# Second layer's mixer matrix spread over the convolution, message columns paired, transposed copies on ScalarE

## The chip, the cores and the metric

The kernel runs as one program on 1 core of one Trainium2 chip. The metric is the device time of one execution in microseconds, the median of three runs. Of the kernel before these gave 3021.57, 3025.67 and 3026.47 us, median 3025.67 us.

## The reference, cut to what matters

A two-layer graph network on 3125 nodes of 256 features and 53125 edges. The change is in the second layer and in two places that only move a copy. The second layer computes, on normed rows `xn`:

```python
# _L1_gnn_ref: messages of every edge, summed by destination
s0 = src[:, :64]; s1 = src[:, 64:].reshape(-1, 64, 3)
out0 = alpha * (einsum('ei,io->eo', s0 * a0, w_00_0) + inv_sqrt3 * einsum('eim,em,io->eo', s1, a1, w_11_0))
out1 = alpha * (einsum('ei,io,em->eom', s0, w_01_1, a1) + einsum('eim,io->eom', s1 * a0, w_10_1))
messages = concatenate([out0, out1.reshape(-1, 192)]) * msg_rad
agg = segment_sum(messages, edge_dst) / 4
# _L1_mix_ref: linear attention, no softmax
p_attn = einsum('bhnd,bhne->bhde', k, v) / seq_len
out = einsum('bhnd,bhde->bhne', q, p_attn) ... @ Wfc.T + bfc
# x = x + gnn(xn) + mix(xn), then a gated mixture of 4 experts whose gates come from x_norm @ W_gat and a graph attention
```

The mixer is linear in its rows, so it is one 256 x 256 matrix G and one bias row for all nodes; both follow from the Gram matrix of `xn`.

## The kernel before, in words

Nodes lie in NB = 25 blocks of 128 rows (`k.X`, 128 x 25 x 256, stays in SBUF). Each stage is an `nc.Block`: five engines with their own instruction lists, joined by semaphores inside and by a barrier at the end. All products are f32; one f32 product shows as two MATMUL records. The stages that matter here, in order of time:

- `combine0` (L1263), 1003 to 1062 us: per block ScalarE norms the rows (L595), TensorE turns them (L1297), VectorE copies the turned rows out of PSUM (`keep`, L1329), TensorE multiplies by `Ws` (L1307), VectorE scales, adds twice and takes statistics (L1339 to L1343, L475), GpSimd adds the bias (L1289).
- `experts0` (L1380), 1278 to 1524 us: eight experts in turn on TensorE. GpSimd meanwhile sends columns of the sorted pairs for the later gate graph to HBM by indirect DMAs (`Scatter`, L1995, one column each, L2009), paced by expert (`pace`). 281 columns are spread over the stages by `SORT_SCATTER = 6`, `RETURN_SCATTER = 28`, `GRAM_SCATTER = 30`, `MIX_SCATTER = 34` and the end, 36, in units of eight columns: 176 in `experts0`, 16 in `return0`, 32 in `gram1`, 9 in `mixer_matrix1`.
- `gram1` (L2132), 1602 to 1650 us: norms, the table `x_tab` of gather rows, the Gram matrix in `sums`, edge factors; GpSimd issues 4 gathers and 32 scatters. VectorE also clears the accumulator of the next stage (L2229, 128 x 12800).
- `mixer_matrix1` (L2241), 1651 to 1675 us: G and its bias row, five dependent steps of TensorE products and VectorE copies; GpSimd issues the last 9 scatters.
- `convolve` (L2318), 1675 to 2251 us: 55 turns of U = 8 steps of 128 edges. GpSimd gathers 128 source rows per step into a ring of RT = 4 turns (L2345). ScalarE makes `msg` (L2369, L2371), VectorE the one-hot matrix (`mark`, L2383), the products with the three angular factors (`weigh`, L2393), their sum (`join`, L2401, L2403) and the adds of two halves of each step's result into `acc` (`add`, L2413). TensorE does one 128 x 512 product per step (L2358) over R = 4 banks. GpSimd may run up to four turns ahead of the others.
- `combine1` (L2431), 2251 to 2368 us: per block ScalarE copies the sums and norms the rows (L2464, L595); TensorE turns both (L2483 two, L2485 four), multiplies by G (L2496) and by a 512 x 256 matrix `c_w` laid out from the four 64 x 64 weights with zeros between (L2498); VectorE copies both turned tiles (L2537, L2538), adds (L2548), takes statistics. The bias is added by GpSimd (L2473), one block behind each norm, and after block 9 its queue holds the nine gathers of `Steps.gather` (L239). `Steps` prepares the gate graph: `count`, `widen`, `cuts` after block 9, `gather`, `mark` after block 19, `flip`, `settle`.
- `gate_rows` (L2570), 2371 to 2418 us: per block a norm, two transposes (L2611), two copies of the same turned rows (L2639, L2640), a product of 16 columns (L2621), and five small VectorE instructions for the gate scores (L2651 to L2656). SP stores rows and loads expert weights.

The order inside a block that matters most, `combine1` on TensorE:

```python
turned_block(b + 1, (j + 1) % B5)      # waits normed b+1, kept
pe.wait_ge(kept, b + 3)
for c in range(KC): matmul(ps_o[j % 2][:, 0:D], xT[:, j, c, :], G[:, c, :], ...)
for c in range(4):  matmul(ps_o[j % 2][:, 0:D], aT[:, j, c, :], w[:, c, :], ...)
```

## Time and profile before

| | us |
|---|---|
| median of three runs | 3025.67 |
| the profiled execution's own time | 3023.47 |
| its span | 3021.7 |
| PE / DVE / ACT / POOL busy | 2281.1 / 2035.0 / 1375.9 / 1641.5 |
| `combine0` | 58.5 |
| `experts0` | 246 |
| `gram1` + `mixer_matrix1` | 73.8 |
| `convolve` | 575.7 |
| `combine1` | 117.1 |
| `gate_rows` | 46.5 |

Times are microseconds unless marked ns. PE is TensorE's products, PEld its weight loads, DVE VectorE, ACT ScalarE, POOL GpSimd, SP SyncE; "POOLq" and "SPq" are queues. L12 is a line of the kernel before. Stages are separated by barriers, so a microsecond saved on whatever ends a stage moves all that follows.

### The profile page before, as it was taken

The numbers are of one execution on the slowest core, as the hardware profiler recorded it, in microseconds if no ns is written. First come the engines' busy times: TensorE is split into PE (matmuls) and PEld (weight loads), VectorE is DVE, ScalarE is ACT, GpSimd is POOL, SyncE is SP. The second block draws the span as 40 slices with busy tenths as digits, with TensorE's granted clock in tenths as the row PEclk, the third lists the DMA queues.
The fourth block names the chain that finished last, engine by engine and source line by source line (L and its number), as shares of the span: only waits on it lengthen the run. The fifth ranks groups of instructions, "written<-read, shape, count | busy, mean of one in ns | idle before, by whom it ended". The sixth has DMA issues, their size and how long they took to land. (4 is left out here: it accounts for less than half of the span.)

```text
span 3021.7 us, 41600 instructions
## 1 busy us (share of the span) xinstructions
PE 2281.1 (75%) x11076; PEld 1512.9 (50%) x11076; DVE 2035.0 (67%) x4208; ACT 1375.9 (46%) x4369; POOL 1641.5 (54%) x1754
## 2 busy tenths in 40 slices
PE   3997777777777656699965578777778788888785
PEld 2554455555555455556623223222337677777664
DVE  4564899999999888701075699999984722222586
ACT  0221566666666244321242588888972122222232
POOL 1544766666664204567776677777752077777200
PEclk8998788888888855599976799999989689989898
DMA  3212766666664022233232233333321211111004
GB/s 105 54 41 80 217 192 197 195 193 193 195 193 140 1 58 73 58 88 94 87 85 62 82 105 105 103 104 105 105 63 16 61 37 36 32 37 37 17 1 182
DMA packets 165629, 289.12 MB, mean 96 GB/s; under 512 B 55933, under 2 KB 99970, under 8 KB 165407
## 3 DMA queue, kind: packets, MB, share of 16 engines
q0 software_dynamic: 79344, 187.14, 22.8%
q1 hardware_dynamic: 73906, 80.60, 8.6%
q10 hardware_dynamic: 12156, 18.72, 1.7%
q8 instruction: 102, 1.67, 0.2%
q14 instruction: 121, 0.98, 0.1%
HBM read 250.08 MB, written 36.25 MB: 95 GB/s over the span
## 5 line engine op out<-in xcount | busy, mean ns | idle before, releaser
L949 POOL DMA_INDIRECT at_kv<-kv_tab,e_src x440 | 431.9, 981 | 265.5 <-PE at_a L1066 152.4
L2358 PE MATMUL cv_ps<-cv_msg,cv_hot 128*128 128x512 f32 x880 | 431.1, 632 | 145.3 <-DVE acc L2413 126.5
L2345 POOL DMA_INDIRECT cv_x<-x_tab,e_src x440 | 423.7, 963 | 147.7 <-issue 98.8
L2794 POOL DMA_INDIRECT gs_h<-h_tab,fc_q x312 | 295.1, 946 | 184.9 <-issue 93.6
L2358 PEld LDWEIGHTS cv_ps<-cv_msg,cv_hot 128*128 128x128 f32 x880 | 162.0, 198 | 414.1 <-ACT cv_msg L2371 252.6
L2009 POOL DMA_INDIRECT pairs<-gating_pair,gating_place x281 | 275.9, 982 | 149.0 <-issue 66.5
L2371 ACT ACTIVATE cv_msg<-cv_x,factors 128x64 f32<-128x64 f32 x1320 | 356.5, 333 | 0.0
L2413 DVE TENSOR_TENSOR acc<-acc,cv_ps 128x256 f32 x880 | 306.9, 412 | 6.5 <-PE cv_ps L2358 3.8
L2369 ACT ACTIVATE cv_msg<-cv_x,factors 128x256 f32<-128x256 f32 x440 | 217.8, 495 | 122.6 <-DMA cv_x<-x_tab,e_src 122.6
L1066 PE MATMUL at_a<-at_kv,at_hot_e 128*128 128x264 f32 x880 | 252.9, 416 | 13.9 <-ACT at_hot_e L993 9.9
L1041 PE MATMUL at_q<-q_parts,at_hot_n 128*128 x1320 | 228.2, 329 | 42.5 <-DVE at_hot_n L1128 21.1
L2751 ACT ACTIVATE gs_x_hid<-gs_x_h,x_b 128x128 f32<-128x128 f32 x320 | 91.5, 369 | 303.9 <-PE gs_x_h L2718 303.9
L2728 PE MATMUL gs_x_y<-x_w,gs_x_hid 128*128 128x256 f32 x640 | 171.6, 419 | 51.6 <-DVE gs_y L2758 51.5
L1041 PEld LDWEIGHTS at_q<-q_parts,at_hot_n 128*128 128x128 bf16 x1320 | 147.3, 113 | 112.7 <-issue 61.2
L1066 PEld LDWEIGHTS at_a<-at_kv,at_hot_e 128*128 128x128 f32 x880 | 163.7, 207 | 47.3 <-ACT at_hot_e L993 19.0
L1003 ACT ACTIVATE at_kv<-at_kv 128x32 f32<-128x32 f32 x864 | 185.6, 306 | 0.0
L1167 DVE TENSOR_TENSOR acc<-acc,at_a 128x528 f32 x220 | 154.0, 700 | 39.5 <-PE at_a L1066 31.9
L2871 DVE TENSOR_REDUCE gs_as_dst<-gs_d 128x32 f32<-128x96 f32 x39 | 10.1, 258 | 250.7 <-DMA gs_h<-h_tab,fc_q 250.7
L2728 PEld LDWEIGHTS gs_x_y<-x_w,gs_x_hid 128*128 128x128 f32 x640 | 128.7, 210 | 73.7 <-issue 46.9
L2718 PE MATMUL gs_x_h<-xnT,x_w 128*128 128x128 f32 x1280 | 161.0, 283 | 0.0
L2718 PEld LDWEIGHTS gs_x_h<-xnT,x_w 128*128 128x128 f32 x1280 | 157.9, 199 | 2.7
L1138 DVE TENSOR_TENSOR at_kv<-at_kv,at_q 128x512 f32<-128x512 f32 x220 | 147.2, 680 | 15.9 <-DVE at_ends L1240 6.1
(546 smaller groups left out, 4437.9 us busy)
## 6 DMA issues: line engine op xcount, KB each, us to landing
x_space<-in_L_ffn_w SPq DMA_DIRECT2D x16, 1024.0 KB, 7.0
at_rel_row<-e_rel_rows SPq DMA_DIRECT2D x55, 256.0 KB, 4.5
experts_out<-gs_y ACTq DMA_DIRECT2D x20, 512.0 KB, 2.7
x_y<-experts_out SPq DMA_DIRECT2D x20, 512.0 KB, 6.9
at_kv<-kv_tab,e_src POOLq DMA_INDIRECT x440, 3.7
cv_x<-x_tab,e_src POOLq DMA_INDIRECT x440, 2.8
kv_tab<-p_qkv SPq DMA_DIRECT2D x25, 256.0 KB, 2.0
gs_h<-h_tab,fc_q POOLq DMA_INDIRECT x312, 2.4
```

The source lines that it names most:

```text
L949: nc.gpsimd.indirect_dma_start(out=kv[:, t % (RING * Q4), 0:2 * D], out_offset=None, in_=kv_tab, in_offset=bass.IndirectOffsetOnAxis(ap=e. ...
L1041: ins = nc.tensor.matmul(ps_q[dd % 3][:, u, :], hot_n[:, t // Q4 % NHOT, t % Q4 * P:(t % Q4 + 1) * P], q_parts[:, ds(b, 1), n, :].rearrang ...
L1066: nc.tensor.matmul(to, hot_e[:, t // Q4 % NEDGE, t % Q4, :], kv[:, t % (RING * Q4), D:2 * D + H1], start=(u == 0), stop=(u == 1), skip_gro ...
L2009: nc.gpsimd.indirect_dma_start(out=pairs, out_offset=bass.IndirectOffsetOnAxis(ap=place_i[:, c:c + 1], axis=0), in_=pair[:, c, :], in_offs ...
L2345: nc.gpsimd.indirect_dma_start(out=xg[:, i % RT, u, :], out_offset=None, in_=x_tab, in_offset=bass.IndirectOffsetOnAxis(ap=e.src[:, t:t + ...
L2358: nc.tensor.matmul(ps[u % R][:, :], hot[:, i % 2, u, :], msg[:, i % 2, u, :], start=True, stop=True).then_inc(summed, 1)
L2369: nc.scalar.activation(msg[:, h, u, 0:D], xg[:, i % RT, u, :], ACT.Copy, scale=factor[:, t:t + 1, 0])
L2371: ins = nc.scalar.activation(msg[:, h, u, D + m * M:D + (m + 1) * M], xg[:, i % RT, u, 0:M], ACT.Copy, scale=factor[:, t:t + 1, 1 + m])
L2413: v.tensor_tensor(row, row, ps[u % R][:, n * D:(n + 1) * D], ALU.add).then_inc(added, 1)
L2718: ins = self.nc.tensor.matmul(self.ps_h[e % 2][:, f * P:(f + 1) * P], self.x1.w1[:, e, c, f * P:(f + 1) * P], self.xnT[:, c, b * P:(b + 1) ...
L2728: ins = self.nc.tensor.matmul(self.ps_y[e % 2][:, 0:D], self.hid[:, e % 2, f, :], self.x1.w2[:, e, f, :], start=(f == 0), stop=(f == FX // ...
L2794: nc.gpsimd.indirect_dma_start(out=hg[:, i % RT, u, :], out_offset=None, in_=h_tab, in_offset=bass.IndirectOffsetOnAxis(ap=e.src[:, i * U ...
```

## The change

Seven parts, all in one diff:

1. `combine0`: the copy of the turned rows moves from VectorE to ScalarE, which norms block b + 1 before it copies block b.
2. Scatters: `RETURN_SCATTER` 28 to 30, so `experts0` issues 192 (16 more); `return0` 16 as before; `gram1` the last 25 (7 fewer); `MIX_SCATTER` is gone.
3. `gram1` no longer clears `acc`; `convolve` does, before its first `mark`.
4. `mixer_matrix1` is gone. A class `NodePart` cuts its work and the product of every block with G into 57 phases (7 for the matrix and the bias, 2 for each block), laid over slots 1 to 105 of 110, two slots a turn. TensorE's part stands after step 3 or 7 of a turn, ScalarE's copy one half turn later, VectorE's add to `k.X` after `add` of step 2 or 5. One PSUM bank serves all.
5. `msg` is laid out in pairs of 64 columns, so each of the four turned tiles of `acc` meets one of two 128 x 64 weights.
6. `combine1`: no norm, no rows turned, no product with G, no copy of `acc` (TensorE turns `acc` directly); four products of 64 columns a block; ScalarE makes the one copy left; four weight loads of DMA instead of eight; GpSimd adds all 25 bias rows first, then gathers; buffers three deep.
7. `gate_rows`: the score weights are multiplied into the 24-column weight once; per block ScalarE makes one copy, VectorE two small ones.

```diff
         def _(act):
-                for i in range(0, NB // B5):
-                    for j in range(B5):
-                        act.wait_ge(turned, i * B5 + j + 1)
-                        normed_block(nc, k, act, i * B5 + j, xn[:, j, :], normed)
...
+                norm(0)
+                for b in range(NB):
+                    norm(b + 1)
+                    act.wait_ge(turned, b + B5 + 1)
+                    if b >= B5:
+                        act.wait_ge(done, b - B5 + 1)
+                    nc.scalar.activation(xT[:, b % B5], ps_t[b % B5 % 2][:, 0:D].rearrange("p (c t) -> p c t", t=P), ACT.Copy).then_inc(kept, 1)
```

```diff
 # scatters, and the head of gram1's and convolve's changes
-RETURN_SCATTER = C2 // U - 8
+RETURN_SCATTER = C2 // U - 6
 GRAM_SCATTER = RETURN_SCATTER + 2
-MIX_SCATTER = GRAM_SCATTER + 4
...
-        scatter = Scatter(s, "g1_sc_", GRAM_SCATTER, MIX_SCATTER)
+        scatter = Scatter(s, "g1_sc_", GRAM_SCATTER, C2 // U)
...
-                v.memset(acc[:, :, :], 0.0).then_inc(emptied, 1)
```

```diff
+class NodePart:
+    MIX = 7
...
+        phases = self.MIX + 2 * NB
+        self.phase_at = {1 + p * (slots - 4) // phases: p for p in range(phases)}
...
+    def multiply(self, pe, slot):
+        p = self.phase_at.get(slot)
+        if p is None:
+            return
...
+        if 0 < p <= self.MIX:
+            pe.wait_ge(self.kept, p)
...
+        elif (p - self.MIX) % 2 == 0:
+            b = (p - self.MIX) // 2
+            pe.wait_ge(self.normed, b + 1)
+            if b:
+                pe.wait_ge(self.added, b)
+            for c in range(KC):
+                ins = nc.tensor.transpose(bank[:, c * P:(c + 1) * P], self.xn[:, b % 2, c * P:(c + 1) * P], k.ident[:, :])
+        else:
+            b = (p - self.MIX) // 2
+            pe.wait_ge(self.kept, self.MIX + b + 1)
+            for c in range(KC):
+                ins = nc.tensor.matmul(bank[:, D:2 * D], self.xT[:, b % 2, c, :], self.G[:, c, :], start=(c == 0), stop=(c == KC - 1))
+        ins.then_inc(self.made, 1)
+    def keep(self, act, slot):
...
+        if p < self.MIX or (p - self.MIX) % 2 == 0:
+            act.wait_ge(self.made, p + 1)
...
+    def add(self, dve, slot):
...
+        dve.wait_ge(self.made, p + 1)
+        self.nc.vector.tensor_tensor(self.k.X[:, b, :], self.k.X[:, b, :], self.bank[:, D:2 * D], ALU.add).then_inc(self.added, 1)
```

```diff
 # convolve: TensorE, ScalarE, VectorE
                         nc.tensor.matmul(ps[u % R][:, :], hot[:, i % 2, u, :], msg[:, i % 2, u, :], start=True, stop=True).then_inc(summed, 1)
+                        if u == 3:
+                            node.multiply(pe, 2 * i)
+                    node.multiply(pe, 2 * i + 1)
...
+                        parts = msg[:, h, u, :].rearrange("p (r x i) -> p x r i", x=2, i=M)
...
+                        if u == 3:
+                            node.keep(act, 2 * i - 1)
+                    node.keep(act, 2 * i)
...
+                node.clear()
+                v.tensor_copy(angles, factor[:, 0:T1, 1:4]).then_inc(kept, 1)
                 v.tensor_copy(counted, k.count_row[:, 0:P]).then_inc(kept, 1)
-                dve.wait_ge(kept, 2)
+                v.memset(acc[:, :, :], 0.0).then_inc(kept, 1)
+                dve.wait_ge(kept, 3)
...
                     add(i, blocks, 1, 2)
+                    node.add(dve, 2 * i - 1)
                     join(i + 1)
-                    add(i, blocks, 3, 4, 5, 6, 7)
+                    add(i, blocks, 3, 4, 5)
+                    node.add(dve, 2 * i)
+                    add(i, blocks, 6, 7)
```

```diff
 # combine1
+                for b in range(NB):
+                    act.wait_ge(turned, b + 1)
+                    if b >= 3:
+                        act.wait_ge(done, b - 2)
+                    nc.scalar.activation(aT[:, b % 3], ps_a[b % 3][:, :].rearrange("p (c t) -> p c t", t=P), ACT.Copy).then_inc(kept, 1)
...
                 for b in range(NB):
-                    pool.wait_ge(normed, b + 1)
...
+                    nc.gpsimd.tensor_tensor(k.X[:, b, :], k.X[:, b, :], bias, ALU.add).then_inc(biased, 1)
+                st.gather(pool)
...
+                def mix(b):
+                    pe.wait_ge(kept, b + 1)
+                    if b >= 3:
+                        pe.wait_ge(added, 2 * (b - 2))
+                    for c in range(4):
+                        ins = nc.tensor.matmul(ps_o[b % 3][:, c * M:(c + 1) * M], aT[:, b % 3, c, :], w[:, min(c, 1), :], start=True, stop=True,
+                                               skip_group_check=True)
+                    ins.then_inc(done, 1)
...
+                for b in range(NB):
+                    turn(b + 2)
+                    mix(b)
+                    if b == B5 - 1:
+                        st.widen(pe)
+                    if b == 4 * B5 - 1:
+                        st.flip(pe)
...
 # gate_rows
+                for b in range(NB):
+                    turned_block(b + 2)
+                    pe.wait_ge(kept, b + 1)
...
+                    for c in range(KC):
+                        ins = nc.tensor.matmul(ps_h[b % B5][:, 0:GW + H2], xnT[:, c, b * P:(b + 1) * P], w[:, c, :], start=(c == 0),
+                                               stop=(c == KC - 1))
...
+                    dve.wait_ge(done, b + 1)
+                    v.tensor_copy(h[:, j, :], ps_h[j][:, 0:GW]).then_inc(ready, 1)
+                    v.tensor_copy(as_dst[:, b, :], ps_h[j][:, GW:GW + H2]).then_inc(taken, 1)
```

## Rows read from the trace of the kernel before

**Rows 1.** Busy time by stage; columns: stretch, its length, PE, PEld, DVE, ACT, POOL, PEclk, DMA share, GB/s
```profile
1003.00:1061.50 58.50, 39.93 (x152) 28.27 (x151) 54.98 (x127) 14.33 (x25) 18.47 (x25) 0.85 0.00 1
...
1601.70:1650.60 48.90, 29.07 (x124) 22.79 (x124) 31.23 (x64) 14.60 (x25) 35.73 (x36) 0.78 0.25 74
1650.60:1675.50 24.90, 20.42 (x48) 10.65 (x48) 3.89 (x15) 0.00 (x0) 8.65 (x9) 0.56 0.01 1
...
1700.00:2200.00 500.00, 382.70 (x788) 143.59 (x788) 467.41 (x985) 445.42 (x1581) 379.75 (x395) 0.97 0.36 104
...
2251.20:2368.30 117.10, 90.76 (x460) 78.04 (x460) 56.47 (x135) 27.59 (x50) 26.31 (x34) 0.88 0.09 13
...
2371.50:2418.00 46.50, 36.48 (x152) 29.75 (x152) 37.95 (x181) 14.32 (x25) 0.00 (x0) 0.50 0.36 96
```

**Rows 2.** `combine0`, groups: shapes, count | busy, mean ns | idle before, releaser
```profile
L1329 DVE COPY c_xT<-c_t 128x256 f32<-128x256 f32 x25 | 10.1, 408 | 0.0
```

**Rows 3.** `experts0` on POOL, in order of time: start, length, what
```profile
1292.24 0.96 POOL L2009 DMA_INDIRECT pairs<-gating_pair,gating_place  x1 [0.71 <-PE x_h L1448]
...
1519.04 0.96 POOL L2009 DMA_INDIRECT pairs<-gating_pair,gating_place  x1 [0.30 <-issue]
1524.13 0.10 POOL L1544 MEMSET re_top<- 128x1 f32 x1 [4.13 <-POOLq L1400]
```

**Rows 4.** `gram1`, `mixer_matrix1` and the start of `convolve` on POOL
```profile
1638.84 0.96 POOL L2009 DMA_INDIRECT pairs<-gating_pair,gating_place  x1 [0.31 <-issue]
...
1647.69 0.96 POOL L2009 DMA_INDIRECT pairs<-gating_pair,gating_place  x1 [0.31 <-issue]
1651.19 0.96 POOL L2009 DMA_INDIRECT pairs<-gating_pair,gating_place  x1 [2.54 <-SPq L2257]
...
1676.16 0.98 POOL L2345 DMA_INDIRECT cv_x<-x_tab,e_src  x1 [13.88 <-SPq L2336]
```

**Rows 5.** VectorE at the end of `gram1` and the start of `convolve`
```profile
1630.10 10.72 DVE L2229 MEMSET acc<- 128x12800 f32 x1 [2.62 <-issue]
...
1675.54 2.00 DVE L2414 COPY cv_factors<-factors 128x1760 f32<-128x1760 f32 x1 [0.58 <-PEq L2257]
...
1687.78 1.76 DVE L2393 TENSOR_TENSOR cv_s1w<-cv_x,cv_factors 128x1536 f32<-128x1536 f32 x1 [8.79 <-DMA cv_x<-x_tab,e_src]
```

**Rows 6.** `convolve` from 1800 to 2000, groups, columns as in the second group
```profile
L2345 POOL DMA_INDIRECT cv_x<-x_tab,e_src x159 | 153.6, 966 | 48.5 <-issue 35.7 <-ACT cv_msg L2371 12.2 <-DVE cv_s1w L2393 0.6
...
L2393 DVE TENSOR_TENSOR cv_s1w<-cv_x,cv_factors 128x1536 f32<-128x1536 f32 x20 | 35.1, 1754 | 10.7 <-DMA cv_x<-x_tab,e_src 10.6
```

**Rows 7.** `combine1` on PE, in order of time
```profile
2260.77 1.06 PE L2485 MATMUL c_a<-ident,c_ac 128*128 128x128 f32 x4
...
2269.58 0.60 PE L2485 MATMUL c_a<-ident,c_ac 128*128 128x128 f32 x4
2270.01 1.03 PE L2496 MATMUL c_o<-G,c_xT 128*128 128x256 f32 x4
...
2347.11 0.90 PE L231 MATMUL s_turned<-ident,s_scratch 128*128 128x128 f32 x3 [5.79 <-DVEq L305]
```

**Rows 8.** `combine1`, who waited for whom: total, times, longest
```profile
DVE X L2548 <- POOL X L2473: 10.2, 1, 10.2
```

**Rows 9.** Busy time and granted clock, columns as in the first group, of three short stretches
```profile
2261.00:2263.00 2.00, 2.00 (x11) 1.76 (x10) 1.09 (x3) 1.12 (x2) 2.00 (x4) 0.50 0.00 0
2263.00:2265.00 2.00, 2.00 (x10) 1.78 (x10) 1.90 (x4) 1.12 (x2) 2.00 (x4) 1.00 0.00 0
1080.00:1090.00 10.00, 9.48 (x89) 9.19 (x87) 8.62 (x13) 7.57 (x20) 0.00 (x0) 0.50 0.28 62
```

**Rows 10.** `gate_rows` on PE, one block back to back, in order of time
```profile
2380.55 0.87 PE L2621 MATMUL gr_ps_h<-gat_w,gr_xT 128*128 128x16 f32 x4
2381.27 0.67 PE L2611 MATMUL gr_t<-ident,gr_xn 128*128 128x128 f32 x2
```

**Rows 11.** Expert products of the gate stage on PE
```profile
2500.28 1.95 PE L2718 MATMUL gs_x_h<-xnT,x_w 128*128 128x128 f32 x16
```

More of the change, by code:

```diff
@@ L2320, in convolve @@
+def convolve(nc, k, e, x_tab, factor, sums, acc, spaces):
     turns = T1 // U
@@ L2398, in join @@
                         return
[L2399 removed]
+                    last = msg[:, i % 2, :, M:2 * M]
                     dve.wait_ge(freed, i + 1)
```

426 lines of the change are left out of this document (185 added, 241 removed).

## The prediction

> **What bounds the kernel now.** I read the busy time by stage first [rows 1], since a mean over 3021.7 us hides five different limits, then the order of time at each stage's start and end, then who waited for whom. Each touched stage ends on another engine. `combine0` is VectorE's: 54.98 of 58.50 us busy [rows 1]. `experts0` is TensorE's, but GpSimd has little room: its scatters go at 0.96 + 0.30 = 1.26 us each, and the last began 5.1 us before the next stage [rows 3]. `gram1` ends on GpSimd: its last scatter begins at 1647.69, and the next block's first scatter 3.50 us later [rows 4], while VectorE's late work is a memset that ends at 1640.8 [rows 5]. `mixer_matrix1` is a chain of small steps in which TensorE is busy 20.42 of 24.90 us at clock 0.56 [rows 1]. `convolve` is GpSimd's: 159 gathers took 153.6 us of work and 35.7 us of issue, with only 12.8 us of waits for the other engines, (153.6 + 48.5) / 159 = 1.27 us each or 10.17 us a turn; ScalarE and VectorE start turns by waiting for gathered rows (10.6 us of such waits on VectorE in 200 us) [rows 6]. `combine1` is TensorE's once it runs (2.00 of 2.00 us busy at clock 1.00) [rows 9], plus gaps of which the largest single one is 10.2 us in which VectorE waits for bias rows that stand behind nine gathers in GpSimd's queue [rows 8]. `gate_rows` is VectorE's and TensorE's at clock 0.50 [rows 1].
>
> **The change, part by part.** *`combine0`.* VectorE loses 25 copies of 0.408 us [rows 2], 10.2 us of busy time. Pipelined they are worth less, because an instruction's start overlaps the end of the last: I take 0.33 each, 8 us. ScalarE has 14.33 us busy in 58.5 [rows 1] and takes 10 more without becoming the limit. TensorE does 39.93 / 25 = 1.6 us a block at clock 0.85 against the 1.8 that VectorE keeps. Gain 8, between 4 (TensorE at half clock in more blocks) and 10.
>
> *Scatters.* `experts0` gets 16 more. Its fourth scatter begins at 1292.24 [rows 3]; the other 188 at 1.264 each (the seven steps from 1638.84 to 1647.69 in rows 4) put the last at 1529.9 if nothing paces them. The pace doesn't help or hurt: 24 scatters take 30.3 us, an expert takes (1519.04 - 1292.24) / 173 x 22 = 28.8. So GpSimd, hidden until now, ends the stage: 1529.9 + 3.5 [rows 4] = 1533.4 against 1524.13 [rows 3], a loss of 9. Between 0 (if half of them were to find gaps, which no row shows) and 12. `gram1` has seven fewer: its last begins where the 25th does now, 1638.84 instead of 1647.69 [rows 4], a gain of 8.9, provided VectorE doesn't end it; the memset leaves it, so its copies of the sums, now at 1640.7 behind the memset that began at 1630.10 [rows 5], come 10.7 us earlier. The nine of `mixer_matrix1` vanish with it.
>
> *`mixer_matrix1`.* The whole block goes: 24.9 us [rows 1]. What it did is paid for inside `convolve`.
>
> *`convolve`.* The path is GpSimd's 440 gathers, which the change doesn't touch; the others have room, and a ring of four turns decouples them. Load per turn of 10.17 us, old from rows 1 (500 us are 49.2 turns), new by division over 55 turns: VectorE 467.41 / 49.2 = 9.5, plus 25 adds of 0.42 = 0.2, so 9.7. ScalarE 445.42 / 49.2 = 9.05, plus 25 norms of 14.32 / 25 = 0.57 [rows 1] and 25 copies at about 0.41 [rows 2] and the matrix's seven, 0.5, so 9.6. TensorE 382.70 / 49.2 = 7.8, plus the matrix, 20.42 x 0.56 = 11.4 us at full clock [rows 1], and 25 times two transposes (0.22) and four records of 256 columns (1.03) [rows 7], 0.8 in all, so 8.6. All stay under 10.17, the nearest by 0.5. The waits that the phases add: ScalarE waits for TensorE's phase, with `msg` of the next steps behind it, for which TensorE waits; it stands half a turn after the phase and I find it late by up to 2 us, made up in the next turn that has no copy. TensorE's transposes wait for VectorE's add of the block before, with the next products behind them; 48 of the 56 distances between phases are two slots, where the add is long done. The memset of 10.72 us now precedes the first `mark`: VectorE's start at 1675.54 leaves 12.2 us until the first rows are there [rows 5], of which copies and `mark` take 3.5, so it is late by some 2 us, and the first phases by up to 8. Both are lags of the consumers, not of GpSimd, and at 0.5 us a turn they are gone after 20 of 55 turns. I cost the stage at 0. If that cover is gone, every 0.1 us over 10.17 costs 5.5. Bounds -2 (no row gives the gathers less work) to +60.
>
> *`combine1`.* Four DMAs instead of eight let the weights in about 5 us after the stage's start, not 9. A block then is four transposes, 2270.01 - 2269.58 = 0.43 us [rows 7], and eight records of 64 columns. No row has these at full clock: 128 columns take 1.95 / 16 = 0.12 [rows 11], which is the upper bound; at half clock 16 columns take (2381.27 - 2380.55) / 4 = 0.18 [rows 10], which halved is 0.09. I take 0.10, nearer to the wide one, so 1.25 us a block against about 3.25 now. VectorE has two small adds and statistics, about 1.0; ScalarE one copy, 27.59 / 50 = 0.55 [rows 1]. Measured from the stage's start: weights 4.7; three blocks of transposes and one of products at half clock 4.0; 19 blocks at 1.25 and `widen`, 24.5: block 19 is done at 33.2. After block 9, at 21.7, `cuts` takes 2.5; nine gathers at 1.26 and a landing of about 2 us put the windows at 37.5, so now `mark` waits for the gathers, not for the blocks: this is what becomes late next. Bias rows are no longer behind them. `mark` 4.8, `flip` at half clock 1.4, the last five blocks 6.9 (TensorE has stood still and starts slowly, as at 2347.11 [rows 7]), and 2 us of VectorE: 52.5. Gain 117.1 [rows 1] - 52.5 = 64.6.
>
> The LDWEIGHTS section of the Trainium skill's page "TensorE: Matmul & The Clock Gate" puts a weight load at columns / 1.2 ns, 107 ns for 128. By that estimate a block is 1.29 us and the stage 1 us longer; no row here separates the two.
>
> *`gate_rows`.* VectorE falls from seven instructions a block to two of about 0.17; then TensorE's 2 transposes and 4 records at half clock, 0.72 [rows 10] and 0.45, set 1.17 us a block. ScalarE has a norm and a copy, 0.9. With 3 us of start and 2 of end, 34.5 against 46.5 [rows 1]: gain 12, between 8 (a store behind 1 MB of weights) and 16 (if the clock rises).
>
> **Sum.** 8 - 9 + 8.9 + 24.9 - 0 + 64.6 + 12 = 109.4. The profiled execution took 3023.47 us, 2.2 below the median of the runs; 3023.5 - 109.4 = 2914.
>
> **Rivals.** *Half clock in `combine1`.* In a stretch of the router with transposes and products of 8 columns TensorE was busy 9.48 of 10 us and the clock stayed at 0.50 [rows 9]; narrow products may not lift it, and the new stage has 64 columns where it had 256. Then a block is 0.86 (1.06 for four with its tail [rows 7]) + 8 x 0.18 = 2.3 us, block 19 is done at 53, the stage ends at 71: 18.7 later, 2933 us. Against it: the step from 0.50 to 1.00 at 2263.0 came when TensorE had done nothing but transposes since 2260.3 [rows 7, 9], and the new stage begins with twelve of them. The same page's section on the PE-mode transpose says that transposes don't count as activity; by that rule the rival would be likelier than not. The row at 2263.0 speaks against that rule, so I leave it at 0.17.
>
> *`convolve` becomes VectorE's.* Order matters more than load: a phase in which TensorE waits for an add or VectorE for a late product costs VectorE time. It decides from (10.17 - 9.7) x 55 = 26 us in all. With 1 us lost at each of 57 phases the turn is 10.7, the stage 31 longer, 2945. For it: slack of 5%; against: banks are refilled four steps ahead, and VectorE's adds stand after the phase. 0.17.
>
> *Slower than before.* Same place, but each phase empties the pipeline: ScalarE, TensorE and VectorE hand one bank round, and `msg`, the products and `acc`'s adds stand behind every hand-over. At 3 us a phase (a product, a copy, an add and their signals) 171 us go to 55 turns, 3.1 each; 9.7 + 3.1 = 12.8 a turn, 145 us more, 3059. It turns the gain round from 2.4 us a phase. Only 0.03, since two slots, 10 us, lie between a phase and the next.
>
> *More than forecast*: records of 64 columns at 0.06, `gate_rows` at full clock, scatters that find room: 2896. 0.08.
>
> **How the numbers follow.** The forecast has 0.55, its own range 2903 to 2927 from the bounds of `combine0`, scatters and `gate_rows`. The range takes in the half clock whole and the near half of `convolve`'s rival, and at the low end half of the extra gain: 2898 to 2946. About 0.2% (6 us) is what a measurement of this kernel can tell from no change; only the last of the slow cases and small mishaps of unnamed size reach it: faster 0.96, same 0.01, slower 0.03.
>
> **What would show it.** `experts0` with GpSimd's last scatter near 1530 and TensorE idle before the barrier; `gram1` ending some 9 us sooner; the first convolution gather at about 1676 - 8 + 9 - 34 = 1643; 10.1 to 10.2 us between the starts of `weigh` with waits for DMA on VectorE after some 20 turns; in `combine1` a granted clock of 1.00 until `mark` and POOL's gathers as VectorE's releaser; 1.17 us a block in `gate_rows`. Wrong if GpSimd waits for `weigh` or for ScalarE in `convolve` for more than the 12.8 us per 200 of now, or if `combine1`'s clock stays at 0.50.

## The result and the profile after

The changed kernel takes 2924.66 us (median of four runs, 2923.32 to 2928.94) against 3025.35 us: a ratio of 0.9674, 95% interval 0.9659 to 0.9688. The forecast was 2914, the range 2898 to 2946. The gain is 100.7 us, 8.7 less than worked out.

Its profiled execution has a span of 2921.6 us. First the stages: stretch, its length, then busy time of PE, PEld, DVE, ACT and POOL with counts, granted clock, DMA share, GB/s. They stand in the order `combine0`, `experts0`, `gram1`, 500 us of `convolve`, `combine1`, `gate_rows`; most of them answer to [rows 1].

```profile
1002.20:1053.70 51.50, 35.22 (x150) 26.62 (x150) 48.89 (x102) 21.17 (x50) 19.44 (x25) 0.86 0.00 1
1274.00:1524.60 250.60, 229.42 (x832) 150.35 (x832) 23.52 (x48) 42.79 (x64) 181.95 (x190) 0.96 0.29 84
1602.00:1644.00 42.00, 27.73 (x124) 22.09 (x124) 21.09 (x66) 14.48 (x25) 28.88 (x30) 0.83 0.28 86
1700.00:2200.00 500.00, 397.13 (x946) 167.18 (x945) 473.34 (x1005) 462.19 (x1631) 380.56 (x393) 0.99 0.36 104
2221.70:2282.00 60.30, 38.40 (x309) 37.50 (x309) 33.87 (x111) 15.15 (x26) 26.09 (x34) 0.80 0.17 23
2282.00:2318.00 36.00, 30.72 (x152) 29.78 (x152) 8.68 (x62) 22.38 (x51) 0.00 (x0) 0.50 0.51 130
```

The table compares marks that both traces have (first and last starts of named instructions), so that each stretch holds a stage with its barrier.

| stretch | before | after | change | forecast |
|---|---|---|---|---|
| `combine0`, bias copy to last add | 57.9 | 51.1 | -6.7 | -8 |
| `experts0`, first product to next stage | 240.7 | 250.7 | +10.0 | +9 |
| `gram1` and `mixer_matrix1`, to the first convolution gather | 74.4 | 41.8 | -32.6 | -33.8 |
| `convolve`, first gather to last add | 574.6 | 577.3 | +2.7 | 0 |
| `combine1`, to the first product of `gate_rows` | 120.9 | 60.6 | -60.2 | -64.6 |
| `gate_rows` | 48.1 | 36.0 | -12.1 | -12 |
| the rest of the kernel behind it | 601.95 | 603.6 | +1.6 | 0 |

The rows add up to 97.3 of the 100.1 us between the two profiled spans; the other 2.8 lie ahead of `experts0`, outside `combine0`, where nothing was edited. The last row holds no edit either; in the kernels run below, most of which leave it alone too, it was 600.0 to 607.2. What lies ahead of `experts0` varied between 1272.3 and 1279.0 us in kernels that have this part unchanged. So single stages are compared by their own marks; only sums of several microseconds are read from the medians.

`experts0` ends on GpSimd. On POOL (start, length, what, and in brackets the idle time before it and what ended it) three rows, and under them TensorE's last work in the stage and the first behind it:

```profile
1281.01 0.96 POOL L2010 DMA_INDIRECT pairs<-gating_pair,gating_place  x1 [10.24 <-PE x_h L1450]
...
1522.06 0.96 POOL L2010 DMA_INDIRECT pairs<-gating_pair,gating_place  x1 [0.30 <-issue]
1524.62 0.10 POOL L1546 MEMSET re_top<- 128x1 f32 x1 [1.60 <-POOLq L1402]
...
1495.17 14.08 PE L1459 MATMUL x_y<-x_space,x_hid 128*128 128x256 f32 x64 [0.76 <-ACT x_hid L1479]
1524.81 2.09 PE L2099 MATMUL re_ef_h<-ef_emb,ef_w 20*128 20x512 f32 x8 [15.56 <-PEq L1402]
```

TensorE is done at 1509.3 and stands still for 15.6 us while the last scatters go out. Also to be seen: GpSimd waited 10.24 us for TensorE ahead of its third scatter (issued at 1281.01).

`combine1`, rows of TensorE and VectorE:

```profile
2226.55 2.82 PE L2542 MATMUL c_a<-ident,acc 128*128 128x128 f32 x12 [5.71 <-DVE c_w L2568]
2229.16 1.80 PE L2550 MATMUL c_o<-c_w,c_aT 128*128 128x64 f32 x8
2232.08 0.61 PE L2542 MATMUL c_a<-ident,acc 128*128 128x128 f32 x4
2232.53 1.00 PE L2550 MATMUL c_o<-c_w,c_aT 128*128 128x64 f32 x8
2233.37 0.60 PE L2542 MATMUL c_a<-ident,acc 128*128 128x128 f32 x4
...
2262.63 0.36 DVE L285 CAST s_from_node<-s_edges 128x384 f32<-128x384 int32 x1 [3.92 <-DMA s_edges<-pairs,e_chunk]
...
2267.59 0.90 PE L231 MATMUL s_turned<-ident,s_scratch 128*128 128x128 f32 x3 [10.69 <-DVEq L305]
```

A block takes 2233.37 - 2232.08 = 1.29 us, of which the eight records of 64 columns take 2233.37 - 2232.53 = 0.84, 0.105 each. VectorE then waits 3.92 us for the windows, the edge lists that GpSimd's nine gathers bring, and TensorE stands still for 10.69 us in all until the marked windows can be turned.

### The profile page after: what moved, and what is told of

It is laid out like the page before. It is cut to its first block and busy times, and to the rows that moved or that the text cites. A ratio compares the mean times of both kernels' runs of the same rounds, so it can differ in the third digit from the quotient of the medians.

```text
span 2921.6 us, 41520 instructions
## 1 busy us (share of the span) xinstructions
PE 2224.1 (76%) x11075; PEld 1495.1 (51%) x11076; DVE 1978.0 (68%) x4041; ACT 1396.4 (48%) x4454; POOL 1642.7 (56%) x1754
## 5 line engine op out<-in xcount | busy, mean ns | idle before, releaser
L2413 PE MATMUL cv_ps<-cv_msg,cv_hot 128*128 128x512 f32 x880 | 420.6, 613 | 128.3 <-DVE acc L2475 79.9
L1041 PE MATMUL at_q<-q_parts,at_hot_n 128*128 x1320 | 229.6, 330 | 41.8 <-DVE at_hot_n L1128 21.1
```

Source lines behind the costliest of these rows:

```text
L1041: ins = nc.tensor.matmul(ps_q[dd % 3][:, u, :], hot_n[:, t // Q4 % NHOT, t % Q4 * P:(t % Q4 + 1) * P], q_parts[:, ds(b, 1), n, :].rearrang ...
L2413: nc.tensor.matmul(ps[u % R][:, :], hot[:, i % 2, u, :], msg[:, i % 2, u, :], start=True, stop=True).then_inc(summed, 1)
```

## Experiments

Ratios are to the kernel before, measured beside it; a difference to the changed kernel (0.9674) in microseconds is the difference of ratios times 3025. Each ratio is good to about 5 us either way, a difference of two to about 7. The stretches between marks are good to about 1: `convolve` took 577.2 to 578.5 in the seven profiled kernels that leave it alone, its gathers 559.2 to 560.5. Only `combine1` varies more. In the nine kernels that leave it alone it took 60.0 to 60.9 in six and 65.1 to 65.7 in three (experiments 3, 4 with two copies, and 6), and the clock is what differed; see the rivals in the next section.

### 1. The scatters' split put back

```diff
-RETURN_SCATTER = C2 // U - 6
+RETURN_SCATTER = C2 // U - 8
```

> The changed kernel with only the split of the scatters put back: the expert stage has 176 again instead of 192, and the Gram stage 41 instead of 25. Theory (GpSimd ends both stages, every scatter is worth 1.26 us where it is exposed): the expert stage falls from 250.7 to about 240.7 us, since TensorE's own last product then ends it; the Gram stage, from its first instruction to the convolution's first gather, grows from 41.8 by 16 x 1.26 = 20.2 to 62.0; together 10 us slower than the changed kernel, about 2935. Rival (the 10 us that the expert stage lost come from the traffic of the scatters or from the clock, not from their number at the end): the expert stage stays within 2 us of 250, and the whole is 18 to 20 slower, 2944.

Measured: 0.9713 (0.9697 to 0.9730), 11.8 slower than the changed kernel. `experts0` 240.5, from `gram1` to the first gather 62.0, all else unchanged within 1 us. Both numbers of the theory to 0.2 us. In `gram1`, which GpSimd ends, a scatter costs its 1.26 us whole: 16 of them 20.2. Moved into `experts0`, the same 16 cost 10.2: the last scatter came 12.8 us later in the stage, the rest went into gaps of the paced queue.

### 2. Scatters of `experts0` without the pace

```diff
-                scatter.run(nc, k, pool, pairs, pair, place_i, pace=pace)
+                scatter.run(nc, k, pool, pairs, pair, place_i)
```

> The changed kernel, where the scatters of the expert stage no longer wait for TensorE's marks but are issued as fast as GpSimd can. Theory (with 192 scatters the stage is GpSimd's, and its waits for TensorE, 10.2 us before the third scatter and 7.3 in all after it, are paid in full): the second scatter is at 1269.8, 190 more at 1.264 put the last at 1510, just behind TensorE's last product at 1509.3; the stage ends at 1514 instead of 1524.6, 10.5 us faster, 2914. Rival (the pace protects the experts' row and weight loads from the scatters' traffic): TensorE waits for weights, its last product slips by more than 5 us, and the gain is below 5 or turns into a loss.

Measured: 0.9638 (0.9622 to 0.9654), 10.9 faster than the changed kernel, 2914.24 us. `experts0` takes 240.4 us. Its last scatter and the start of the next stage on POOL, and the stage in one row (columns as in the first table of rows):

```profile
1513.18 0.96 POOL L2010 DMA_INDIRECT pairs<-gating_pair,gating_place  x1 [0.30 <-issue]
1516.55 0.10 POOL L1546 MEMSET re_top<- 128x1 f32 x1 [2.40 <-POOLq L1402]
...
1276.10:1516.50 240.40, 229.41 (x832) 150.48 (x832) 23.51 (x48) 42.84 (x64) 179.65 (x188) 0.98 0.30 88
```

The scatters now start in step with the stage, not 10 us into it, and TensorE's busy time is as before, 229.4: the scatters' traffic slowed nothing that shows. With 192 scatters the stage is as long as with 176 and the pace (240.5 in experiment 1), so the loss that the forecast booked for the 16 scatters was the pace's, not theirs.

### 3. The phases left out of the convolution

```diff
         assert len(self.phase_at) == phases
+        self.phase_at = {}
...
-                dve.wait_ge(node.added, NB)
-                dve.wait_ge(node.kept, node.MIX)
```

> The changed kernel with all 57 phases of the node work left out of the convolution: the mixer matrix and its product with the rows are not computed, and X lacks that part. Theory (the stage is GpSimd's, phases lie in the others' slack): the stretch from the convolution's first gather to its last, 559.8 us, shrinks by no more than the 3.3 that it grew, and the whole is 0 to 4 us faster, 2921 to 2925. Rival (convolution is VectorE's with the phases in, order costs more than load): 10 us or more faster, and GpSimd's waits for ScalarE's messages, 15.5 us in 200, fall to under 5.

Measured: 0.9670 (0.9651 to 0.9689), 1.2 faster. From first to last gather 558.1, to the last add 576.3, so 57 phases cost 1.8 and 1.0 us in a stage of 577, little more than the spread of unchanged kernels. Both profiles from 1800 to 2000, with the phases and without them:

```profile
1800.00:2000.00 200.00, 159.05 (x378) 67.79 (x379) 189.92 (x408) 185.54 (x656) 152.19 (x158) 0.98 0.36 104
```

```profile
1800.00:2000.00 200.00, 148.91 (x316) 54.94 (x315) 186.95 (x393) 177.06 (x629) 152.09 (x158) 0.99 0.36 104
```

Without them PE is busy 10.1 us less, ACT 8.5 and DVE 3.0; GpSimd does what it did.

### 4. One and two more VectorE copies a turn

```diff
+        spare = [s.sb(f"cv_spare{q}", [P, D]) for q in range(2)]
...
                     node.add(dve, 2 * i - 1)
+                    for q in range(1):          # the second kernel: range(2)
+                        v.tensor_copy(spare[q][:, :], held[:, 0:D])
                     join(i + 1)
```

> The changed kernel with one more VectorE copy of 128 x 256 from PSUM in each of the 55 turns of the convolution, about 0.41 us; its target is not read. Theory (a turn of VectorE holds 9.66 of 10.17 us): 10.07 still fits under GpSimd's turn, the stage grows by 0 to 5 us. Rival (VectorE is already the one that sets the turn): 55 x 0.41 = 22 us slower, 2947.

> The changed kernel with two more such copies a turn, 0.82 us. Theory: a turn of VectorE is now 9.66 + 0.82 = 10.48, over GpSimd's 10.17 by 0.31, so the stage grows by 0.31 x 55 = 17 us, and GpSimd's idle time moves from issue to waits for VectorE or ScalarE. Rival (VectorE sets the turn already): 45 us slower. A second rival (starts of instructions overlap, so that there is more room than the busy time says): under 8.

Measured: one copy 0.9704 (0.9687 to 0.9721), last add at 582.7, so 5.4 later (9 by the medians); two copies 0.9716 (0.9699 to 0.9732), last add at 586.3, 9.0 later (13 by the medians). Three `weigh` of the second kernel in a row, where no wait for rows is left:

```profile
1989.97 1.75 DVE L2456 TENSOR_TENSOR cv_s1w<-cv_x,cv_factors 128x1536 f32<-128x1536 f32 x1
...
2000.06 1.74 DVE L2456 TENSOR_TENSOR cv_s1w<-cv_x,cv_factors 128x1536 f32<-128x1536 f32 x1
...
2010.47 1.74 DVE L2456 TENSOR_TENSOR cv_s1w<-cv_x,cv_factors 128x1536 f32<-128x1536 f32 x1
```

A turn of VectorE is 10.09 us, and 10.41 with a node add; over the stage that would be 10.24 on average, and a few turns are longer. A copy of 0.41 us costs 0.33 in a row of others, so without the two it is 9.58: the forecast had 9.7. With two copies VectorE ends the stage: 15.9 us to the first `weigh`, 55 turns of 10.24, and a remainder of 7.2 (the longer turns and the last adds, taken from this kernel) make 586.3. Turned round, VectorE ends it from (577.3 - 15.9 - 7.2) / 55 = 10.08 us a turn; the room per turn is 0.50 us (forecast: 0.47). So the theory's mechanism held and its 17 us were too many, by the overlap of starts that the second rival named; that rival's own figure, under 8, was too low. One copy, 9.9 a turn, stays below that point and still cost 5.4 us, just over the theory's 0 to 5. Neither theory has a reason for it; the gathers themselves had grown, to 564.8 from first to last.

### 5. What lengthens the gathers

All 440 gathers in one row each, kernel before, changed kernel, and the one with one copy more (minimum, median, maximum in ns, first and last start):

```profile
L2345 POOL DMA_INDIRECT cv_x<-x_tab,e_src x440: 942/949/1423, 1676.2 to 2232.7; - x147
```

```profile
L2400 POOL DMA_INDIRECT cv_x<-x_tab,e_src x440: 942/946/1459, 1644.0 to 2203.8; - x147
```

```profile
L2401 POOL DMA_INDIRECT cv_x<-x_tab,e_src x440: 942/949/1453, 1648.6 to 2213.4; - x147
```

In none of them is there a gap over 0.35 us between two gathers: GpSimd never waits. What differs are 43 to 53 gathers that take more than 1 us. Their excess over 0.95 sums to 6.4 us before, 10.6 in the changed kernel, 7.6 without phases, 14.7 with one copy more; in seven kernels with this stage unchanged it was 9.9 to 11.3. Of the 5.0 us that one copy added to the gathers' stretch 4.1 are such excess; most of the rest is a median of 0.949 instead of 0.946, whose cause is open. One of them, on POOL, and what VectorE did beside it:

```profile
1853.07 0.95 POOL L2400 DMA_INDIRECT cv_x<-x_tab,e_src  x1 [0.30 <-ACT cv_msg L2431]
1854.32 1.44 POOL L2400 DMA_INDIRECT cv_x<-x_tab,e_src  x1 [0.30 <-issue]
...
1853.54 0.68 DVE L2463 TENSOR_TENSOR cv_msg<-cv_s1w 128x512 f32<-128x512 f32 x1
1854.26 0.69 DVE L2465 TENSOR_TENSOR cv_msg<-cv_msg,cv_s1w 128x512 f32<-128x512 f32 x1
1854.86 1.41 DVE L2475 TENSOR_TENSOR acc<-acc,cv_ps 128x256 f32 x4
```

The gather starts 0.06 us into the second addition of `join` and ends at 1855.76, 0.81 us behind that addition's end at 1854.95. The same holds for all 45 long gathers of the changed kernel: each starts inside one of the two additions of `join`, the only VectorE instructions in the loop with both operands in SBUF (`mark` and `weigh` read one of theirs from PSUM), and ends 0.81 or 0.82 us after that one's end. Fifty-five gathers start inside such an addition. Of the ten that stay at 1 us or under, nine start in its last 0.19 us, where by the same sum little or nothing is left to pay, and one starts together with it. A gather that is under way when an addition begins is not lengthened (42 of them, at most 0.949). Beside `mark`, `weigh`, the adds to `acc` or the clearing of `acc` none is lengthened. So what the stage pays depends on where the joins fall against the gathers, and an edit to VectorE's list can move them. The next kernel tests the link itself.

```diff
-                    v.tensor_tensor(last, s1w[:, :, 0, :], s1w[:, :, 1, :], ALU.add).then_inc(chain, 1)
-                    dve.wait_ge(chain, i + 1)
-                    v.tensor_tensor(last, last, s1w[:, :, 2, :], ALU.add).then_inc(built, 1)
+                    v.tensor_reduce(last, s1w[:, :, :, :].rearrange("p u m i -> p u i m"), AX.X, ALU.add).then_inc(built, 1)
```

> The changed kernel, where VectorE sums the three weighed parts of a message in one reduction over 1536 elements instead of two additions of 512 that each read two operands from SBUF. In every profile so far GpSimd never waits in the convolution; what differs is the time of about 45 gathers that take up to 1.46 instead of 0.95 us, and nearly every one of them overlaps such an addition and ends about 0.1 us behind it (excess of the long gathers: 6.3 us in the kernel before, 10.5 in the changed one, 14.7 with one copy a turn more). Theory (an addition with both operands in SBUF holds GpSimd up, a reduction with one doesn't): the excess goes to under 2 us, the gathers' stretch falls from 559.8 to 551, but VectorE's turn grows by 0.35 to about 10.08, just over GpSimd's 10.02, so that VectorE's last add ends 4 to 7 us earlier, not 9: about 2919. Rival (the reduction holds GpSimd up as well, or the lengthening has to do with VectorE being busy in any way): the excess stays at 8 or more, and the stretch at 558 or longer.

Measured: 0.9660 (0.9642 to 0.9678), 4.2 faster than the changed kernel by the medians, an interval that holds zero. The gathers:

```profile
L2400 POOL DMA_INDIRECT cv_x<-x_tab,e_src x440: 942/946/983, 1646.7 to 2195.6; - x147
```

```profile
1905.58 0.41 DVE L2368 TENSOR_TENSOR X<-X,cv_node 128x256 f32<-128x256 f32 x1
1905.91 1.90 DVE L2463 TENSOR_REDUCE cv_msg<-cv_s1w 128x512 f32<-128x1536 f32 x1
1907.74 3.39 DVE L2473 TENSOR_TENSOR acc<-acc,cv_ps 128x256 f32 x10
...
1800.00:2000.00 200.00, 158.74 (x380) 67.00 (x378) 198.52 (x380) 186.53 (x661) 151.26 (x161) 0.99 0.36 106
```

Not one gather of 440 is longer than 0.983 us, though 74 start inside the reduction alone (at most 0.949), and first to last takes 548.9 instead of 559.8: the cause is shown. Nor is it peculiar to additions. In the first layer's attention, which no run here edits, the changed kernel has 30 gathers (`at_kv`) over 1 us that start inside a multiplication with both operands in SBUF (L1156); they take up to 1.96 us and end 0.81 to 0.82 behind it. In `convolve` the stage gains nothing, since the reduction takes 1.83 in its row where the two additions took 1.33: VectorE, busy 198.52 of 200 us, now ends it at 577.1. Taking 15.9 to the first `weigh` and the remainder of 7.2, its turn is 10.07, as expected. What the expectation (a last add 4 to 7 us earlier) left out was that remainder on top of 55 turns: with it VectorE's own end lies 0.2 us from the end that the long gathers had set.

The Trainium skill's page "SBUF — State Buffer", section "Who interferes with whom", says that a VectorE instruction with two SBUF inputs contends with a GpSimd instruction that reads SBUF, and that a reduction never does; both agree with the 45 gathers and the 0. The same section infers that descriptor generation isn't touched by such an addition; here gathers issued by GpSimd took up to 1.459 instead of 0.946 us, and the measurement decides.

### 6. The clearing of acc back in the Gram stage

```diff
                 v.tensor_copy(sums[0:1, 2, 0:D], ps_row[0:1, 0:D]).then_inc(moved, 1)
+                v.memset(acc[:, :, :], 0.0).then_inc(moved, 1)
                 dve.wait_ge(copied, G1)
-                dve.wait_ge(moved, 1)
+                dve.wait_ge(moved, 2)
...
-                v.memset(acc[:, :, :], 0.0).then_inc(kept, 1)
-                dve.wait_ge(kept, 3)
+                dve.wait_ge(kept, 2)
```

> The changed kernel with the clearing of acc (10.7 us on VectorE) put back into the Gram stage, but behind VectorE's last copies there, at about 1633, where it ends at 1644, beside GpSimd's last scatters. Theory (the cleared accumulator stood ahead of the first weigh, which ran 4 us late, and that lag is what the convolution's last add, 2.7 us later than in the kernel before, shows): the first weigh comes at 11.6 us behind the first gather instead of 15.9, the Gram stage grows by 0 to 2 us, the convolution shrinks by 0 to 3; together between 2 faster and 2 slower. Rival (the lag is caught up at once and the 3.3 us come from the phases): convolution unchanged at 577, and the whole slower by what the Gram stage grows.

Measured: 0.9696 (0.9680 to 0.9712), 6.7 slower. `gram1` grew by 3.8, the first `weigh` came at 11.7, and still the last add came at 581.3, 4.0 later, with 1.4 of it in the gathers. So the late first `weigh` is not why `convolve` grew, and there the rival was right; but it also expected the stage unchanged, which it wasn't. The other 2.6 us fall behind the last gather and weren't settled. `combine1` took 5.0 longer in the profiled execution; its clock rose 12.8 us after the first transpose, where it was 4.3 in the changed kernel.

### 7. Cuts earlier, flip later in combine1

```diff
-                    if b == B5 - 1:
+                    if b == 0:
                         st.widen(pe)
...
                 turn(0)
-                turn(1)
                 st.cuts(dve)
+                turn(1)
                 turn(2)
```

> The changed kernel, where combine1 works out the cuts behind block 4 instead of block 9, and the wide row is spread behind block 0. Nothing is added or removed. Theory (the mark of the windows waits for the gathers, 3.92 us of idle VectorE at 2258.7): GpSimd's nine gathers start when its bias adds end, 2240 instead of 2247, so their windows are there about 2257, and the mark starts right behind block 19: the stage takes 56.8 instead of 60.7, 3.9 faster, 2920.8. Rival (another cost ends the wait, for example the store of the block row on the DMA rings, or GpSimd and VectorE slow each other down when gathers and adds overlap): gain under 1.5.

Measured: 0.9655 (0.9638 to 0.9671), `combine1` 59.4, only 1.3 shorter, though the wait for the windows is gone. The start of `mark` in this kernel, and TensorE from the turn of the windows to its last product, here and in the changed kernel:

```profile
2254.48 0.22 DVE L2575 TENSOR_TENSOR X<-X,c_o 128x64 f32<-128x64 f32 x1 [0.46 <-PE c_o L2550]
2255.22 0.34 DVE L285 CAST s_from_node<-s_edges 128x384 f32<-128x384 int32 x1
...
2260.20:2272.50 12.30, 12.28 (x58) 12.09 (x58) 3.29 (x12) 1.79 (x3) 0.00 (x0) 0.50 0.00 0
```

```profile
2267.60:2276.10 8.50, 8.50 (x58) 8.36 (x58) 3.26 (x12) 1.79 (x3) 0.00 (x0) 0.75 0.00 0
```

The mark starts right behind block 19, 5.1 us earlier in the stage (3.9 expected), but the same 58 records took 12.3 us at a granted clock of 0.50 throughout, where the changed kernel's clock rose on the way and they took 8.5. The clock took back 3.8 of what the wait gave: neither the theory nor its rival had that. That the shorter pause was the reason is not shown. Experiment 3 leaves `combine1` alone, TensorE stood still for 11.6 us ahead of these records, and yet:

```profile
2270.63:2282.96 12.33, 12.32 (x58) 12.13 (x58) 3.29 (x12) 1.79 (x3) 0.00 (x0) 0.50 0.00 1
```

In the other eight kernels with `combine1` unchanged they took 8.0 to 8.9. The next kernel adds the later flip, which leaves TensorE work during the mark:

```diff
-                    if b == 4 * B5 - 1:
+                    if b == 4 * B5 + 2:
                         st.flip(pe)
```

> As the kernel with early cuts, and TensorE turns the marked windows behind block 22 instead of block 19. Theory (TensorE stands still for 10.7 us before the turn although three result banks are free): blocks 20 to 22 are done during the mark, so VectorE adds them as soon as the mark ends, and only 23 and 24 are left: mark from 2258.7 to 2263.5, three blocks of adds at 0.9 each to 2266.2, two more by 2268, the turned windows copied and the last statistics by 2270, against 2278.5: 9 us faster than the changed kernel, 2916. Rival (the last blocks run at half clock whatever the order, because TensorE has stood still before them): 6 us or less.

Measured: 0.9641 (0.9625 to 0.9658), 10.0 faster than the changed kernel; `combine1` 51.8, 8.8 shorter, as the theory had it. With three blocks done before the flip, it doesn't matter that the last two are slow.

```profile
2269.65 0.55 PE L231 MATMUL s_turned<-ident,s_scratch 128*128 128x128 f32 x3 [1.94 <-DVEq L305]
...
2269.76 0.22 DVE L2575 TENSOR_TENSOR X<-X,c_o 128x64 f32<-128x64 f32 x1 [0.21 <-DVE e_src L300]
```

### 8. Products 256 wide in combine1

```diff
-        w = s.sb("c1_w", [P, 2, M])
+        w = s.sb("c1_w", [P, 2, D])
...
-                        ins = nc.tensor.matmul(ps_o[b % 3][:, c * M:(c + 1) * M], aT[:, b % 3, c, :], w[:, min(c, 1), :], start=True, stop=True,
-                                               skip_group_check=True)
+                        ins = nc.tensor.matmul(ps_o[b % 3][:, 0:D], aT[:, b % 3, c, :], w[:, min(c, 1), :], start=(c == 0), stop=(c == 3))
```

> The changed kernel, where each product of combine1 is 256 columns wide, padded with zeros, and the four of a block are added in one bank, as in the kernel before; the node products stay in the convolution. The order of the columns is left as the narrow kernel has it, so the messages are not mixed rightly. This splits the stage's 60 us of gain into what the narrow products bring and what the move of transposes, node products and copies brings. Theory (TensorE ends the stage up to block 19): a block is 0.43 of transposes and 8 records of 0.26, 2.5 us, against 1.28; block 19 is done 23 us later, of which 4 fill the wait for the windows, and the last five blocks take 6 more: 25 us slower than the changed kernel, combine1 at 86, 2950. So the narrow products would be 25 of the 60 and the rest 35. Between 20 and 30 by the time at which the clock rises. Rival (VectorE or the bank hand-over ends the stage, not the products): under 12.

Measured: 0.9721 (0.9705 to 0.9738), `combine1` 78.3, 17.6 longer: below the theory's 20 to 30, above the rival's 12.

```profile
2236.87 0.60 PE L2543 MATMUL c_a<-ident,acc 128*128 128x128 f32 x4
2237.31 1.89 PE L2551 MATMUL c_o<-c_w,c_aT 128*128 128x256 f32 x8
2239.03 0.60 PE L2543 MATMUL c_a<-ident,acc 128*128 128x128 f32 x4
```

A block is 2.16 us, its eight records of 256 columns 1.72, 0.216 each, and not 0.26: that came from a row of four whose displayed length includes a tail. So of the stage's gain of 60.2 us the narrow products bring 17.6, and the rest of the change to it (node work, copies, norms and the order of the bias rows, not separated further) 42.6. A quarter of the columns doesn't cost a quarter: 0.105 us against 0.216.

### 9. combine0 and gate_rows as before

Both functions are put back to the text of the kernel before; of the diff ahead of the prediction this undoes, in short:

```diff
-                    nc.scalar.activation(xT[:, b % B5], ps_t[b % B5 % 2][:, 0:D].rearrange("p (c t) -> p c t", t=P), ACT.Copy).then_inc(kept, 1)
+                    v.tensor_copy(xT[:, j], ps_t[j % 2][:, 0:D].rearrange("p (c t) -> p c t", t=P)).then_inc(kept, 1)
```

> The changed kernel with combine0 and gate_rows as in the kernel before: in both VectorE makes the transposed copies again, and gate_rows works out the two sums of a row for each block instead of once for the weights. Theory (the stages are independent of the others and each gain is its own): combine0 is 6.7 us longer (57.8 against 51.1), gate_rows 12.1 longer (48.1 against 36.0), together 18.8 slower than the changed kernel, 2943.5. Rival (part of the difference between the two profiles is a state of the clock, not the change): under 14 in sum.

Measured: 0.9724 (0.9707 to 0.9741). `combine0` 57.6, 6.5 longer; `gate_rows` 47.8, 11.8 longer: 18.3 by the marks. By the medians it is 15, within the intervals.

### 10. Together

Experiments 2, 5 and 7 in one kernel, with the clearing of `acc` split:

```diff
+                for b in range(NB // 2, NB):
+                    nc.scalar.activation(acc[:, b, :].rearrange("p (a q) -> p a q", q=P), wide(k.ident[:, :].unsqueeze(1), [P, 4, P]), ACT.Copy,
+                                         scale=0.0).then_inc(kept, 1)
...
-                v.memset(acc[:, :, :], 0.0).then_inc(kept, 1)
-                dve.wait_ge(kept, 3)
+                v.memset(acc[:, 0:NB // 2, :], 0.0).then_inc(kept, 1)
+                dve.wait_ge(kept, 3 + NB - NB // 2)
```

> The changed kernel with what the runs before it pointed to: scatters of the expert stage without the pace, cuts worked out after block 4 and windows turned behind block 22 in combine1, one reduction instead of two additions in the convolution, and half of the clearing of acc given to ScalarE, which waits for the first rows there anyway. Theory: expert stage 240.4 (10.3 less), combine1 52 (8.7 less, up to 5 more if the clock rises late), and in the convolution, where with the reduction VectorE alone sets the end, the first weigh comes at 11.6 us instead of 15.9 behind the first gather, so that the last add ends at 573 instead of 577. Sum 23 less, 2902. Rival for the convolution (its end doesn't move with VectorE's start, since TensorE or ScalarE catch up): 577, sum 19, 2906.

Measured: 2907.29 us median, 0.9621 (0.9605 to 0.9637), against 0.9674 for the changed kernel, 16 us faster than it where 19 to 23 were expected. `experts0` 240.3, `convolve` 576.1, `combine1` 57.9.

```profile
1656.72 1.75 DVE L2458 TENSOR_TENSOR cv_s1w<-cv_x,cv_factors 128x1536 f32<-128x1536 f32 x1 [3.21 <-DMA cv_x<-x_tab,e_src]
...
2228.50:2230.50 2.00, 2.00 (x12) 2.00 (x11) 0.67 (x3) 0.26 (x1) 1.30 (x2) 0.50 0.00 0
2234.50:2236.50 2.00, 2.00 (x16) 2.00 (x16) 1.79 (x10) 0.60 (x1) 0.67 (x1) 0.74 0.00 0
```

The first `weigh` did come 4.3 us earlier, but the second waited 3.21 us for the rows of its turn: an early start can't be kept where the next rows aren't there, and the rival held. In `combine1`, where the first transposes are at 2216.50, the clock rose only at about 2235.5, after 19 us, and `combine1` was 6 us longer than in experiment 7's second kernel, which has the same order of work there.

## Why the forecast held, step by step

- *`combine0`*, 8 forecast, 6.7 measured, 6.5 in experiment 9. The term was right in kind; 25 copies were worth 0.27 each, not 0.33.
- *Scatters in `experts0`*, a loss of 9 forecast, 10.0 measured. The last was to start at 1529.9 with the stage beginning at 1283.4, 246.5 after it; it did so at 1522.06 - 1273.9 = 248.2. But "the pace doesn't help or hurt" was the wrong step. It compared rates and took the fourth scatter's start, 1292.24, as given. That start holds the first wait (10.24 us ahead of the third scatter in the changed kernel), which a queue with no slack never makes good: without the pace the loss is gone (experiment 2). So the size came out right because the forecast carried the wait along unseen, not because the pace was harmless.
- *`gram1` and `mixer_matrix1`*: 33.8 forecast, 32.6 measured; first gather at 1643.97 for a forecast of 1643. Experiment 1 confirms 1.26 us a scatter.
- *`convolve`*, 0 forecast, 2.7 lost. That GpSimd sets it and the phases fit beside it held: 57 phases cost 1 to 2 us (experiment 3), near the spread of unchanged kernels, and VectorE's room was 0.50 us a turn (experiment 4). The step at fault is the reading of [rows 6]: the 12.8 us put down as GpSimd's waits for other engines are some forty gaps of 0.3 us like every other between two gathers; it never waits. What varies is the length of its own instruction, through VectorE's additions (experiment 5); the forecast's bounds of -2 to +60 had no term for that. It had also put the first lag down as harmless. In experiments 6 and 10 an earlier first `weigh` brought 1 us or nothing, so that held.
- *`combine1`*, 64.6 forecast, 60.2 measured. By steps from the stage's start: weights 4.9 (4.7), a block 1.283 (1.25), last five blocks 7.2 (6.9), `mark` 4.8 and `flip` 1.3 as said. That the windows would come late, in the place of the bias rows of [rows 8], was right. The term that failed is the landing: from the start of the last gather to the start of `mark` it was 5.6 us, not 1.26 and about 2. That is 2.4 of the 3.4 us by which the windows came late, at 40.9 instead of 37.5; the other 1.0 is a last gather at 35.3 instead of 34.3, since `cuts` took 3.3 instead of 2.5 and began later. The tail was 2.9 instead of 2. The Trainium skill's page "TensorE: Matmul & The Clock Gate", section LDWEIGHTS, gives 107 ns for a load of 128 columns; a record of 64 columns took 0.105 us and one of 256 took 0.216, so at full clock the trace agrees. At a granted clock of 0.50 it doesn't: eight records of 64 columns took 1.60 us in experiment 10, 0.20 each. That it is the load on which a narrow product ends fits these numbers, but no run tested it.
- *`gate_rows`*, 12 forecast, 12.1 measured, and 1.17 us a block at 0.50 as written.

The stages' misses nearly all point the same way, so the total isn't right by cancelling. Of the 9.3 us by which the profiled gain (100.1) fell short of 109.4, the stages above make 10.5, the unedited rest of the kernel 1.6, and the unedited part ahead of `experts0` gave 2.8 back. The forecast's "own range 2903 to 2927" doesn't follow from the bounds that it names, which add up to 2899 to 2925; 2924.66 lies in both.

*The rivals.* Half clock in `combine1`: not in the changed kernel. Its first twelve transposes ran at 0.50 and the clock then rose to 1.00:

```profile
2228.55:2230.55 2.00, 2.00 (x11) 2.00 (x10) 1.76 (x3) 1.19 (x2) 2.00 (x4) 0.50 0.00 0
2230.55:2232.55 2.00, 2.00 (x19) 2.00 (x20) 0.68 (x4) 0.60 (x1) 2.00 (x4) 0.93 0.00 0
```

So narrow products don't keep it down. Whether its twelve transposes had a part in the rise can't be told here, as products stand between them and the rise; the row at 2263.0 in [rows 9] stays the only one that speaks on it. The Trainium skill's page "TensorE: Matmul & The Clock Gate", section on the PE-mode transpose, denies transposes such a part. But the moment of the rise varies. In thirteen kernels with this stage it came 3.7 to 4.8 us after the first transpose in ten, 12.7 and 12.8 in two, 19.1 in one, from the same instructions back to back. What differed ahead of it was the fall: in the ten the clock had gone down to 0.50 2.0 to 3.2 us before the first transpose, in the three only 0.8 to 1.4. TensorE had stood still for 5.7 to 5.8 us before that transpose in twelve of them (6.4 in the one with wide products), so the length of that pause doesn't tell the cases apart; whether the moment could be steered wasn't tried. A block costs 2.45 us at half clock (experiment 10) and 1.28 at full; the late rises made the stage 4.7 to 6.0 us longer, a spread that the forecast's own range didn't name. `convolve` becoming VectorE's: not here, and from 10.08 us a turn on. Each phase emptying the pipeline: no, 57 phases cost under 2 us. Slower was never near.

## What to carry to other kernels

A pace that holds back a queue must be judged by its first wait as well as by its rate: in a queue without slack every wait is paid at the end. Before work is added beside an engine that sets the time, look not only for its waits but for its own instructions growing longer, and for what the neighbour does in those moments. And when a wait is removed in front of TensorE, ask at which clock it starts again; give it blocks to do during the pause rather than only making the pause shorter (both edits together won 8.8 us here, the shorter pause alone 1.3).

## What the runs showed of the hardware

- An indirect DMA issued by GpSimd that starts inside a VectorE addition with both operands in SBUF ends 0.81 us after that addition's end, up to 1.46 instead of 0.95 us; beside a multiplication of that kind it took up to 1.96. One that is already under way isn't lengthened. A reduction over one SBUF operand, a clear, and additions with one operand in PSUM leave it at 0.95.
- TensorE's granted clock rises from 0.50 to 1.00 at a moment that varies from 3.7 to 19.1 us under the same back-to-back work. After a pause of 6 to 12 us five blocks ran either wholly at 0.50 (12.3 us with the turn of the windows, two kernels) or partly (8.0 to 8.9, eight kernels).
- A float32 record of 64 columns costs 0.105 us at full clock and 0.20 at half, one of 256 columns 0.216 at full.
- The nine indirect gathers of `combine1` were usable 5.6 us after the last one was started; in the nine kernels where VectorE waited for them it was 5.2 to 6.5.
